# Row vectors by DMA through a device-memory scratch, and a prologue in pieces

## The reference

```python
xn = _layernorm(x)
# branch 1
q, k, v = qkv[:, :, 0], qkv[:, :, 1], qkv[:, :, 2]        # xn @ W_qkv
q = rotary_embedding(q); k = rotary_embedding(k)           # pairs x[::2], x[1::2]
weights = softmax(where(mask, q k^T / 8, -1e9)); out = weights v; out @ W_out
# branch 2
attn = softmax(q2 k2^T / sqrt(8)); x2 = xn + layernorm((attn v2) @ Wo + bo, g1, be1)
gate_probs = softmax(x2 @ Wg + bg); top 2 of 8 experts; moe = sum(p * (x2 @ We + bexp))
x2 + layernorm(moe, g2, be2)
# result: x + branch 1 + branch 2
```

## Time and profile before

| what | value |
| --- | --- |
| median of 3 runs | 1400.55 us (1398.38 to 1405.91) |
| the profiled execution | 1396.29 us, its span 1394.6 us |
| PE busy | 1242.4 us, 89% of the span |
| DVE busy | 965.9 us, 69% |
| POOL busy | 827.2 us, 59% |
| ACT busy | 801.2 us, 57% |
| mean granted TensorE clock | 0.968 of full |
| DMA q1 (SP) | 35292 packets, 38.33 MB, 11.4% of 16 engines' span |

### The profile page before, as it was taken

One profiled execution on the slowest core, in us unless ns is written; L12 is line 12 of the kernel. 1 busy time (PEld: TensorE's weight loads), 2 busy tenths in 40 slices (PEclk: granted clock), 3 DMA queues, 4 the chain that ended last, 5 costly groups with the idle time before them and its releaser, 6 DMA issues.

```text
span 1394.6 us, 27585 instructions
## 1 busy us (share of the span) xinstructions
PE 1242.4 (89%) x9800; PEld 813.4 (58%) x9800; DVE 965.9 (69%) x2329; ACT 801.2 (57%) x1135; POOL 827.2 (59%) x796
## 2 busy tenths in 40 slices
PE   0688999989999899989998899988999989999994
PEld 0465557655666557756576555765566655775553
DVE  5547656975769658796568955697576975878634
ACT  1366675556655575465855567555665557546660
POOL 0676366772786547592585736667278654759322
PEclk9899999999999999999999999999999999999998
DMA  4111011111111101110011101101011110111000
GB/s 116 44 41 31 16 31 25 31 39 24 24 32 43 28 22 32 25 48 22 18 30 31 46 16 32 31 24 39 24 24 32 40 31 21 33 25 43 12 1 8
DMA packets 38608, 43.04 MB, mean 31 GB/s; under 512 B 10438, under 2 KB 21962, under 8 KB 38348
## 3 DMA queue, kind: packets, MB, share of 16 engines
q1 hardware_dynamic: 35292, 38.33, 11.4%
q10 hardware_dynamic: 3184, 2.95, 0.7%
HBM read 5.60 MB, written 2.10 MB: 6 GB/s over the span
## 4 chain that ended last, share of the span: by engine, by line
PE 48%; DVE 18%; issue 16%; POOL 12%; ACT 3%; SPq 1%; DMA 1%; POOLq 0%; DVEq 0%; ACTq 0%
PE work L922 7%; PE work L947 6%; PE work L835 5%; PE work L1005 4%; PE work L837 4%; PE work L836 4%; PE work L936 3%; DVE work L796 2%; POOL qk_l L449 2%; PE work L898 2%; PE work L977 2%; PE work L968 2%; DVE work L777 2%; DVE fnmax L695 2%; DVE branch L665 2%
## 5 line engine op out<-in xcount | busy, mean ns | idle before, releaser
L695 DVE TENSOR_REDUCE fnmax<-work 128x2 f32<-128x1024 f32 x256 | 303.7, 1218 | 88.4 <-PE work L977 87.0
L524 ACT ACTIVATE fpt<-work 128x1024 f32<-128x1024 f32 x256 | 249.5, 1025 | 98.6 <-PE work L994 97.1
L796 DVE CUSTOM_DVE_ANT_0 work<-work,causal 128x512 f32<-128x512 f32 (+3 forms) x512 | 239.1, 515 | 90.9 <-PE work L898 88.2
L440 POOL TENSOR_TENSOR raw<-raw,cos_t 128x512 f32<-128x512 f32 x128 | 164.1, 1282 | 117.6 <-DMA swapped<-raw 107.4
L457 POOL TENSOR_SCALAR_AFFINE_SELECT pt<-pt 128x256 f32<-128x256 f32 x128 | 49.5, 409 | 298.4 <-ACT pt L573 298.4
L573 ACT ACTIVATE pt<-work 128x1024 f32<-128x1024 f32 (+1 forms) x192 | 164.2, 882 | 61.6 <-PE work L922 60.8
L449 POOL TENSOR_TENSOR qk_l<-raw,qk_h 128x512 fp32r<-128x512 f32 x128 | 163.4, 1285 | 48.9 <-ACT qk_h L555 48.8
L444 POOL TENSOR_TENSOR raw<-raw,swapped 128x512 f32<-128x512 f32 x128 | 164.2, 1283 | 10.0
L441 POOL TENSOR_TENSOR swapped<-swapped,sin_t 128x512 f32<-128x512 f32 x128 | 164.1, 1282 | 0.0
L947 PE MATMUL work<-pt,v 128*64 128x512 f32 (+3 forms) x1024 | 152.0, 439 | 0.5
L549 ACT COPY raw<-work 128x512 f32<-128x512 f32 x128 | 75.7, 592 | 93.0 <-PE work L837 78.5
(11 more groups left out here) (165 smaller groups left out, 2606.4 us busy)
## 6 DMA issues: line engine op xcount, KB each, us to landing
swapped<-raw SPq DMA_DIRECT2D x512, 64.0 KB, 2.0
x_in<-in_L_attn_x_dram SPq DMA_DIRECT2D x8, 256.0 KB, 3.3
out_dram<-x_in SPq DMA_DIRECT2D x8, 256.0 KB, 2.3
fpt<-in_L_attn_W_qkv_dram ACTq DMA_DIRECT2D x1, 1536.0 KB, 6.6
pt<-in_L_ffn_We_dram ACTq DMA_DIRECT2D x1, 512.0 KB, 9.4
wout<-in_L_attn_W_out_dram ACTq DMA_DIRECT2D x1, 512.0 KB, 7.2
pt<-in_rope_dram ACTq DMA_DIRECT2D x1, 192.0 KB, 7.6
qk_bias<-in_L_ffn_bq_dram SPq DMA_DIRECT2D x12, 0.1 KB
```

The lines of the kernel that those rows point to most:

```text
L440: nc.gpsimd.tensor_tensor(raw[:, n % 3], raw[:, n % 3], cos_t[:], ALU.mult)
L524: nc.scalar.activation(fpt[:, i, 2 * r:2 * r + 2].rearrange("p h n -> p (h n)"), bank_of(("fst", b, g, i), 2 * r, 2), ACT.Exp, scale=1.0 / ...
L695: nc.vector.tensor_reduce(fnmax[:, j, 2 * r:2 * r + 2, 0:1], bank_of(("fsm", b, g, j), 2 * r, 2).rearrange("p (f n) -> p f n", f=2), AX.X, ...
L796: ins = nc.vector.tensor_tensor_reduce(out=scores, in0=scores, in1=causal[:, S - n:S], scale=-1.0, scalar=3.0e38, op0=ALU.add, op1=ALU.min ...
```

## The change

Four things change in the attention, and one ahead of it.

- **Maxima.** `nmax` is packed to 128 x 8 and turned by one transpose; ACT copies 8 x 128 to `m_rows`, and a new DMA `mrow` on SP lays them into the two used rows of `max_row`. Likewise `fmT` is one transpose of 128 x 16, `fsub` a copy of 16 x 128, and a DMA `fput` writes the four used rows of `fqk`.
- **Row sums.** `lT`, `fan`, `rT` and `rb` are gone. SP moves the sums by `lc` (two DMAs, to 128 x 8 each), DVE adds and inverts (`inv`), `lr` writes the 4 KB of reciprocals to the device-memory scratch `r_rows`, and `lw` reads them back broadcast into the 128 x 512 `l_wide`, its source with the dimensions 2, 64 (repeated) and 512.
- **Swap.** The rotation pairs stay neighbours, and the swap is two DMAs of 64 partitions, every second one.
- **Order.** The tables START and PSUM are new throughout, with PERIOD 164.78. All new DMAs are on SP's queue, in one order with the swaps.
- **Prologue.** `prepared` is split into semaphores for each load and each derived operand. Statistics of x come first on DVE, then the turned tables, xn, the small heads' weights; W_qkv is loaded, cast and split in three parts of 1024 columns; the experts' weights and the biases come after the first `xl`. POOL takes over the clearing.

```diff
-    "mT": [25.587, 46.296, 75.886, 99.841, 116.019, 138.154, 145.933, 167.735],
...
+    "mT": [106.051, 129.049, 146.803, 165.978, 208.468, 211.948, 225.429, 236.964],
...
-PERIOD = 166.4394
+PERIOD = 164.7835
...
+    "SP": ("swap", "mrow", "lc", "lr", "lw", "fput", "store", "load"),
...
-        nmax = sb("nmax", [P, P + T])
+        nmax = sb("nmax", [P, 2, T])
+        rows = sb("rows", [P, 2 * P], F32R)
+        m_rows, fm_rows = rows[0:2 * T, 0:P], rows[0:T * GH, P:2 * P]
...
+        r_rows = nc.dram_tensor("r_rows", (2, 2, S), F32, kind="Internal").ap()
...
+            sp.dma_start(consts[:], table[:, 0:C_N]).then_inc(table_loaded, 16)
+            sp.dma_start(raw_qk[:, 0:D], wq).then_inc(strips_loaded, 16)
+            sp.dma_start(raw_qk[:, D:2 * D], wk).then_inc(strips_loaded, 16)
             sp.wait_ge(cleared, 1)
+            for k, a in enumerate((bq, bk)):
+                for c in range(1, 4):
+                    sp.dma_start(raw_qk_bias[k * STRIP:k * STRIP + G, :, c * FD:(c + 1) * FD],
+                                 a.rearrange("(g f d) -> g f d", f=GH, d=FD)).then_inc(strips_loaded, 16)
+            sp.dma_start(causal[:, S - P:S], table[:, C_MS:C_MS + P]).then_inc(bias_loaded, 16)
             for name, a in (("bexp", bexp.rearrange("e d -> (e d)")), ("bv", bv), ("bo", bo)):
                 n = E * D if name == "bexp" else D
...
+            sp.dma_start(bg_rows[:], bg.rearrange("(a e) -> a e", a=1).broadcast_to([P, E])).then_inc(bias_loaded, 16)
+            sp.dma_start(x_in[:, 1], x_tiles[1]).then_inc(x_loaded[1], 16)
             for n, a in enumerate((g1, be1, g2, be2)):
-                sp.dma_start(affine[:, n, :], a.rearrange("(a d) -> a d", a=1).broadcast_to([P, D])).then_inc(loaded, 16)
...
-                    for p0 in range(0, P, HB):
-                        p1 = p0 ^ HB
-                        sp.dma_start(swapped[p0:p0 + HB, n % 2], raw[p1:p1 + HB, n % 3]).then_inc(swap_done[n % 2], 16)
+                    for r in range(2):
+                        sp.dma_start(swapped[r:P:2, n % 2], raw[1 - r:P:2, n % 3]).then_inc(swap_done[n % 2], 16)
+                elif kind == "mrow":
+                    c = x_[2]
+                    sp.wait_ge(*after("row", b, c))
+                    sp.wait_ge(*after("st", *ring(1, b, c, NC), 2))
+                    sp.dma_start(max_row[0:P:DH].bitcast(F32), m_rows.bitcast(F32)).then_inc(done["mrow"], 16)
+                elif kind == "lc":
+                    c = x_[2]
+                    sp.wait_ge(*after("lsb", b, c))
+                    sp.wait_ge(*after("inv", *ring(1, b, c, NC)))
+                    for n in range(2):
+                        sp.dma_start(l_part[:, n], l_rows[n * STRIP:P:DH]).then_inc(done["lc"], 16)
+                elif kind == "lr":
+                    c = x_[2]
+                    sp.wait_ge(*after("inv", b, c))
+                    sp.wait_ge(*after("lw", *ring(2, b, c, NC)))
+                    sp.dma_start(r_rows[c % 2].rearrange("h (p j) -> (h p) j", p=DH), l_inv[:]).then_inc(done["lr"], 16)
+                elif kind == "lw":
+                    c = x_[2]
+                    sp.wait_ge(*after("lr", b, c))
+                    sp.wait_ge(*after("div", *ring(1, b, c, NC)))
+                    sp.dma_start(l_wide[:], r_rows[c % 2].unsqueeze(1).broadcast_to([2, DH, S])).then_inc(done["lw"], 16)
+                elif kind == "fput":
+                    g = x_[2]
+                    sp.wait_ge(*after("fsub", b, g))
+                    sp.dma_start(fqk[0:P:STRIP, g % 2, 0].bitcast(F32), fm_rows.bitcast(F32)).then_inc(done["fput"], 16)
...
+            NQ = H * DH
+            act.dma_start(angles, rope.rearrange("(t p) c -> p t c", p=P)).then_inc(rope_loaded, 16)
+            for n in range(3):
+                act.dma_start(raw_qkv[:, n * NQ:(n + 1) * NQ], w_qkv[:, n * NQ:(n + 1) * NQ]).then_inc(wqkv_loaded[n], 16)
+            for dst, src in ((raw_small[:, 0:D], wv), (raw_small[:, D:2 * D], wo), (raw_small[:, 2 * D:2 * D + E], wg)):
+                act.dma_start(dst, src).then_inc(small_loaded, 16)
+            act.dma_start(raw_we, we.rearrange("e d f -> d e f")).then_inc(we_loaded, 16)
+            act.dma_start(wout[:], w_out.rearrange("(c p) n -> p c n", p=P)).then_inc(wout_loaded, 16)
+
+            def cast_part(n):
+                act.wait_ge(wqkv_loaded[n], 16)
+                nc.scalar.copy(wqkv_h[:, n * NQ:(n + 1) * NQ], raw_qkv[:, n * NQ:(n + 1) * NQ]).then_inc(cast, 1)
+
+            act.wait_ge(begun, 1)
+            act.wait_ge(turned, 1)
+            for dst, bank in zip((cos_t, sin_t), TURN_BANKS[0:2]):
+                ins = nc.scalar.copy(dst[:], work[:, bank * BANK:(bank + 1) * BANK])
+            ins.then_inc(rope_ready, 1)
+            cast_part(0)
...
+                    if b == 0:
+                        cast_part(1)
+                        cast_part(2)
+                        act.wait_ge(small_loaded, 16 * 3)
+                        nc.scalar.copy(small_h[:], raw_small).then_inc(cast_small, 1)
+                        act.wait_ge(we_loaded, 16)
+                        nc.scalar.copy(we_h[:], raw_we).then_inc(cast_we, 1)
...
-                    act.wait_ge(*after("st", *ring(1, b, c, NC), 2))
-                    nc.scalar.copy(max_row[:], bank_of(("mT", b, c))).then_inc(done["row"], 1)
+                    act.wait_ge(*after("mrow", *ring(1, b, c, NC)))
+                    nc.scalar.copy(m_rows, bank_of(("mT", b, c))[0:2 * T, 0:P]).then_inc(done["row"], 1)
...
-                    act.wait_ge(*after("rT", *ring(1, b, c, NC)))
+                    act.wait_ge(*after("lc", *ring(1, b, c, NC)))
...
-                elif kind == "fan":
...
-                elif kind == "rb":
...
+            nc.vector.memset(work[:], 0.0).then_inc(prep_dve, 1)
...
+            def turn_tables():
+                turn = turns.rearrange("p a t (h i r) -> p a t h i r", h=2, r=2)
+                dve.wait_ge(rope_loaded, 16)
+                for t in range(T):
+                    sines = angles[:, t, HB:3 * HB].rearrange("p (i r) -> p i r", r=2)
+                    for r in range(2):
+                        nc.vector.tensor_copy(turn[:, 0, t, :, :, r], angles[:, t, 0:HB].unsqueeze(1).broadcast_to([P, 2, HB]))
+                        nc.vector.tensor_copy(turn[:, 1, t, :, :, r], sines[:, :, 1 - r].unsqueeze(1).broadcast_to([P, 2, HB]))\
+                            .then_inc(turn_ready, 1)
+            def strip_weights():
+                dve.wait_ge(begun, 1)
+                dve.wait_ge(table_loaded, 16)
+                dve.wait_ge(strips_loaded, 16 * 8)
...
+                        nc.vector.tensor_tensor(strips_l[:, n, :, c * FD:(c + 1) * FD], src,
+                                                strips_h[:, n, :, c * FD:(c + 1) * FD].bitcast(F32), ALU.subtract)\
+                            .then_inc(strips_ready, 1)
+                bank = TURN_BANKS[2] * BANK
+                dve.wait_ge(turned, 2)
+                nc.vector.tensor_copy(qk_bias[:], work[:, bank:bank + 2 * STRIP].rearrange("p (k g) -> p k g", k=2)[:, :, 0:G])                    .then_inc(prep_dve, 1)
+                dve.wait_ge(prep_dve, 8)
+                for k, low in enumerate((q_low, k_low)):
+                    ins = nc.vector.tensor_scalar(qk_less[:, k], qk_bias[:, k], low, None, ALU.mult)
+                ins.then_inc(columns_ready, 1)
+            def rest_of(n):
+                part = slice(n * H * DH, (n + 1) * H * DH)
+                dve.wait_ge(cast, n + 1)
+                nc.vector.tensor_tensor(wqkv_l[:, part], raw_qkv[:, part], wqkv_h[:, part].bitcast(F32), ALU.subtract)\
+                    .then_inc(qk_ready, 1)
+            def other_weights():
+                rest_of(2)
+                dve.wait_ge(cast_small, 1)
+                nc.vector.tensor_tensor(small_l[:], raw_small, small_h[:].bitcast(F32), ALU.subtract)
+                dve.wait_ge(bias_loaded, 16 * 8)
+                nc.vector.tensor_copy(hi_bias, raw_bias).then_inc(prep_dve, 1)
+                dve.wait_ge(prep_dve, 9)
+                nc.vector.scalar_tensor_tensor(out=biases[:], in0=hi_bias.bitcast(F32), scalar=low_rows, in1=raw_bias,
+                                               op0=ALU.mult, op1=ALU.add)
+                dve.wait_ge(cast_we, 1)
+                nc.vector.tensor_tensor(we_l[:], raw_we, we_h[:].bitcast(F32), ALU.subtract).then_inc(prep_dve, 1)
+                dve.wait_ge(prep_dve, 10)
+                dve.drain().then_inc(prepared, 1)
+                dve.wait_ge(prepared, 1)
...
-                    nc.vector.tensor_tensor(fqk[:, g % 2, 0], bank_of(("fmT", b, g)), fqk[:, g % 2, 0].bitcast(F32),
-                                            ALU.add).then_inc(done["fsub"], 1)
+                    dve.wait_ge(*after("fput", *ring(1, b, g, G)))
+                    nc.vector.tensor_copy(fm_rows, bank_of(("fmT", b, g))[0:T * GH, 0:P]).then_inc(done["fsub"], 1)
...
```

(23 more changed lines are left out.)

422 lines of the change are left out of this document (196 added, 226 removed), and 25 rows, old and new, of tables (PSUM, START).

## The result

The changed kernel takes 1617.6 us (median of four runs, 1611.7 to 1622.6) against 1400.5 (1398.4 to 1405.9) on the same chip: a ratio of 1.154, with a 95% interval of 1.148 to 1.160. That is 217 us slower; I had forecast 1351. The profiled execution's span is 1609.9 us against 1394.6.

A forecast was written before the change was run, and what follows sets the result against it. PE was taken as the bound, 154.4 of 166 us busy. The period became 165.5 - 10.9 + 3 + 4 = 161.6; the span 1394.6 - 15.1 - 23.4 - 11.0 = 1345.1, so 1351 us as median, range 1325 to 1381.

The forecast's parts named there:

- both signs of being wrong: Whole kernel: wrong if the period is outside 158 to 166, or time ahead of the second batch falls under 8 us.
- the step on the row sums: From `ls` to `div`: the DMA chain takes 11.6 us, `lw` 0.6 + 3.3 of it; new waits 4 us a period (0 to 12).
- rival C: Steady periods: waits give back what PE saves; period 165.5, span 1375, time 1381; chance 0.22.
- The 2.0 to 3.3 that I called bounds: Landing of the new 4 KB DMAs: nothing cheaper than the swap's 2.0 us, 3.3 taken from above.
- rival D: `lw` on two DMA engines lands 7 to 8 us later; waits 21 us a period, period 175.6, time 1435; chance 0.20.
- The clock, which my sum held constant: Steady stretch: PE's granted clock read as 0.98; no term for a change in it.
- The PE work removed: Transposes in the attention: four cost 0.45 us; 10.9 us a period go from PE's 154.4.
- the two pairs that fall short: Between `mT` and `st`: two pairs lack 0.6 to 0.8 us for a 3.1 us hop; 3 us a period (1.4 to 8).
- The first part: Up to the second batch: first projection at 18.5 us, first scores 33.1, second batch 125.8; 15.1 us gained.
- The last part: Last batch to the end: PE work to the end of `wo` 193 us for 208, 4 of waits added; 11 us gained.

The follow-up runs named there:

- the series: The changed kernel with, behind its last store, every form of DMA that it uses issued three times alone on SyncE: 1703.6 us, one execution.

## Why the prediction was wrong

**The direction fell with one term.** The period came out at 191.5 us, outside 158 to 166, and the time ahead of the second batch rose by 5 us instead of falling by 8 or more: both signs of being wrong that I had named. In the step on the row sums I took 3.3 us for the landing of `lw`, the load's value in the earlier trace rows. It takes 7.45 alone and 7.50 in the chain above. With `lw` in halves, 2.9, the kernel takes 1381.8, at the upper end of the forecast's own range of 1325 to 1381 and at the time of rival C. The 2.0 to 3.3 that I called bounds were no bounds for this form: all rows behind them are of DMAs whose patterns have 32 rows or more outermost. The lower bound fell too: 4 KB by `lr` took 1.40 us in all, where I had 0.6 + 2.3, and `mrow` 1.62 for 0.6 + 2.0. The landing times of the earlier trace rows run from the issue, so the 0.6 was counted twice. I had said what `lw` might be in rival D and gave it 0.20, although no row spoke against it. That was the wrong choice: where no row has the shape of a new DMA, the price of the mechanism that fits the shape should stand in the sum, and not that of another shape.

**Rival D was right in its mechanism, near in its waits by luck in part, and short in its time.** It put `lw` 7 to 8 us later than 3.3; it was 4.2 later. Its packets were too dear. This is the queue between 1612.92 and 1620 us of the series, with one `lw` under way (columns as in the earlier trace rows):

```profile
q1 hardware_dynamic: 129, 0.26, 10.5%
```

10.5% of 16 engines' 7.08 us are 11.9 us for 128 rows of 2 KB, 0.093 us each and not 0.137. D priced the waits at 21 us a period; PE's idle time rose by 135.1 / 6 = 22.5. That little more than half of the delay gave all of the waits can have to do with the second way of the cost, shown above: other DMAs late behind `lw`. How much of it that way makes was not measured in this order. And D gave a period of 175.6, where it was 191.5. Of the missing 16 us 14 are busy time: D took 10.9 off PE's work, and it rose by 3.5 instead.

**The clock, which my sum held constant.** In the changed kernel the granted clock falls where PE has stood idle. In this timeline of the changed kernel PE waits 2.72 us for `div` and 2.32 for the small heads' maxima, and then eight matmuls of one kind take 1.89 us where the same eight take 1.05 a few microseconds later:

```profile
561.18 0.51 PE L1062 MATMUL work<-fqk 32*128 32x512 f32 x4 [2.72 <-DVE u L900]
...
564.24 0.80 PE L1062 MATMUL work<-fqk 32*128 32x512 f32 x4 [2.32 <-DVE fnmax L783]
...
566.97 1.89 PE L1088 MATMUL work<-fpt,fv 128*9 128x512 f32 x8
...
571.24 1.05 PE L1088 MATMUL work<-fpt,fv 128*9 128x512 f32 x8
```

The granted clock in the stretch of the slow eight, and in one just behind the fast eight (columns as in the earlier trace rows, the number after the last bracket):

```profile
563.30:570.10 6.80, 5.86 (x32) 2.60 (x34) 3.61 (x5) 3.23 (x5) 3.20 (x3) 0.57 0.00 0
573.60:580.40 6.80, 6.67 (x61) 3.05 (x61) 3.33 (x11) 5.93 (x9) 4.46 (x6) 1.00 0.01 2
```

Those are the two levels, 1.2 GHz for most of the first and 2.4 GHz in the second. In the table the clock falls as the idle time grows, 0.97 at 69, 0.93 at 148, 0.87 at 204, but not by the idle time alone: 198 us idle go with 0.91 in the old order, 204 with 0.87 in the new. The changed kernel and the one with `lw` in halves run the same matmuls: 945.3 against 888.6 us busy, so 56.7 us more, on top of 112.9 of idle, and the granted clock is the one thing in these rows that sets the busy times apart. Here each microsecond of new idle time came with half a microsecond of longer work. That is no constant: the same edit in the old order, `lw` in one for `lw` in halves, brought 50.6 us of idle and 7.8 of busy time, 0.15 for one.

**The PE work removed was too dear.** The kernel with the sums alone has the clock of its start (0.97) and 64 transposes a period less: 29.6 / 6 = 4.9 us, where I had 7.2. Four transposes cost 0.31 us among other work, not 0.45; of 10.9 us a period 7.8 remain in the kernel without `lw`, (924.3 - 877.5) / 6. The starts in the earlier trace rows stand beside other kinds of matmul; that their distance held more than the transposes is my guess.

**The maxima.** I gave the hop 3 us a period for the two pairs that fall short. In the changed order `mrow` costs 5.6 us in all by the medians and 10 by the ratios, about 1 a batch at most: sized too high. In the old order `mrow` and `fput` cost 47, and what they saved on top.

**The row sums with the slow form mended.** I gave the whole chain 4 us a period. `lw` in halves alone costs 55 us, 6.9 a batch; in the profiled executions 23.3 of 45.8 us are idle time of the six periods, 11.1 busy time, and the rest lies in the first and the last part.

**The first part** came out: projection 17.00 (forecast 18.5, bounds 15 to 21), first scores 31.2 (33.1). The second batch was forecast at 125.8; with `lw` in halves it is at 127.1. In the changed kernel eight slow `lw` of the first batch turned 14 us of gain into 5 of loss. **The last part**, forecast 11 us shorter, is 4.4 longer with `lw` in halves (265.0), 54 longer with it in one (314.6), and even without `lw` only 3 shorter (257.7). Whether that is for want of work to cover `div` at the end I did not test.

Open: why the sums in the old order leave PE 27 us more idle when 11 us and more lie between copy and `div`. DVE's wait for `lc` (37.3 us, the longest 6.8) is part of it, but no run took it away by itself.

## What to carry to other kernels

Read the pattern of each added DMA as built, both sides, before pricing it: a broadcast whose outermost count is 2 is not priced by a load of the same bytes, and writing it as two DMAs costs one issue. Price a wait on the bound engine with what it does to the clock, here 0.15 to 0.5 of its own length again, and ask what stands behind a slow transfer on the same queue. A hop through memory in place of work on the bound engine wants an order made for it: with the same hops the kernel was 75 us above the prologue alone in one order and 5 in the other. In neither did the hops pay: with `lw` in halves the whole change is faster than the kernel before, but the prologue in pieces without any of the hops is faster still.
